# A linear-attention pass with weights loaded in place, statistics and residuals regrouped, and 1 + exp(-R) on ScalarE

## What is computed

```python
x = x + attn(layernorm(x))
# attn, with K, V, R = time_interp(x) @ W.T + b; 1024 channels
e  = exp(clip(-relu(decay) * t_rem + K, -20, 10));  eu = exp(clip(U + K, -20, 10))
A  = shift(cumsum(e * V)) + eu * V;  B = shift(cumsum(e)) + eu
out = (sigmoid(R) * A / B) @ Wo.T + bo
```

## Time and profile before

| | |
|---|---|
| median of 3 runs | 1482.85 us (1480.77 to 1484.4) |
| profiled execution | 1483.92 us, of which the span from first to last instruction is 1482.1 |
| TensorE matmuls busy | 1372.0 us (93%) |
| VectorE busy | 1198.0 us (81%) |
| ScalarE busy | 735.6 us (50%) |
| POOL busy | 624.6 us (42%) |
| mean granted clock of TensorE | 0.977 of full speed |

### The profile page before, as it was taken

One profiled execution on the slowest core, in us unless ns is written; L12 is line 12 of the kernel. 1 busy time (PEld: TensorE's weight loads), 2 busy tenths in 40 slices (PEclk: granted clock), 3 DMA queues, 4 the chain that ended last, 5 costly groups with the idle time before them and its releaser, 6 DMA issues. The chain is left out here.

```text
span 1482.1 us, 19289 instructions
## 1 busy us (share of the span) xinstructions
PE 1372.0 (93%) x6330; PEld 1115.8 (75%) x6330; DVE 1198.0 (81%) x1914; ACT 735.6 (50%) x1429; POOL 624.6 (42%) x520
## 2 busy tenths in 40 slices
PE   5678999999899998999999989999999889999998
PEld 4556788787787877878877678888888677777776
DVE  4678988998899988999899887777776687888874
ACT  4544555554555545555554434333335265555553
POOL 3433434343343333433434534444445444444452
PEclk9898999999999999999999999999999999999999
DMA  5112000100101001001031236444443312222212
GB/s 174 59 57 71 29 29 29 57 29 1 57 29 57 2 28 57 29 11 46 1 141 66 76 114 237 156 148 145 146 149 114 106 57 86 85 85 85 85 57 86
DMA packets 54549, 114.00 MB, mean 77 GB/s; under 512 B 2768, under 2 KB 7120, under 8 KB 52560
## 3 DMA queue, kind: packets, MB, share of 16 engines
q1 hardware_dynamic: 54480, 113.22, 21.7%
HBM read 88.05 MB, written 25.17 MB: 76 GB/s over the span
## 5 line engine op out<-in xcount | busy, mean ns | idle before, releaser
L779 POOL TENSOR_TENSOR a_ss<-a_ss,a_eu 128x512 f32<-128x512 f32 x64 | 82.5, 1290 | 369.1 <-DVE a_ss L590 369.1
L572 DVE SCALAR_TENSOR_TENSOR bank<-bank,k_or_row 128x510 f32<-128x510 f32 x192 | 132.4, 690 | 93.7 <-ACT k_or_row L458 93.7
L458 ACT ACTIVATE k_or_row<-bank 128x512 f32<-128x512 f32 x192 | 113.7, 592 | 47.3 <-PE bank L81 34.6
L784 POOL TENSOR_TENSOR a_sv<-a_sv,a_euv 128x512 f32<-128x512 f32 x64 | 82.4, 1288 | 111.8 <-DVE a_sv L604 111.8
L364 PE MATMUL bank<-a_wo_hi,a_y_hi 128*128 128x512 f32 x256 | 109.9, 429 | 18.3 <-DVE xres L651 18.3
L478 ACT ACTIVATE bank<-bank,a_nbr 128x510 f32<-128x510 f32 x64 | 42.3, 660 | 152.6 <-DVE bank L572 152.6
L364 PE MATMUL bank<-a_wo_lo,a_y_hi 128*128 128x512 f32 x256 | 105.3, 411 | 0.0
L364 PE MATMUL bank<-a_wo_hi,a_y_lo 128*128 128x512 f32 x256 | 105.3, 411 | 0.0
L488 ACT ACTIVATE bank<-a_ss 128x512 f32<-128x512 f32 x64 | 38.5, 602 | 101.0 <-DVE a_ss L615 101.0
L788 POOL TENSOR_TENSOR a_y_lo<-a_yy,a_y_hi 128x512 fp32r<-128x512 f32 x64 | 83.0, 1297 | 2.3 <-ACT a_y_hi L499 2.3
L1468 POOL TENSOR_TENSOR b_cx_lo<-b_cx,b_cx_hi 128x512 fp32r<-128x512 f32 x32 | 40.5, 1300 | 99.8 <-ACT b_cx_hi L1160 99.8
(11 more groups left out here) (241 smaller groups left out, 4729.3 us busy)
## 6 DMA issues: line engine op xcount, KB each, us to landing
xres<-in_x SPq DMA_DIRECT2D x8, 1024.0 KB, 5.2
x_after_attention<-xres SPq DMA_DIRECT2D x8, 1024.0 KB, 4.3
xin<-x_after_attention SPq DMA_DIRECT2D x8, 1024.0 KB, 5.6
b_ct<-in_ctx_t SPq DMA_DIRECT2D x8, 1024.0 KB, 4.8
b_cx<-in_ctx SPq DMA_DIRECT2D x8, 1024.0 KB, 7.7
xres<-x_after_attention SPq DMA_DIRECT2D x8, 1024.0 KB, 5.6
x_after_cross<-xres SPq DMA_DIRECT2D x8, 1024.0 KB, 4.4
xin<-x_after_cross SPq DMA_DIRECT2D x8, 1024.0 KB, 5.5
```

The lines of the kernel that those rows point to most:

```text
L458: sc.activation(u3[:, :, 1:], ps[m][:, :, :], ACT.Copy, scale=MIX[m]).then_inc(left[m], 1)
L572: ve.scalar_tensor_tensor(out=ps[m][:, :, 0:T - 1], in0=ps[m][:, :, 1:T], scalar=1.0 - MIX[m], in1=u3[:, :, 0:T - 1], op0=ALU.mult, op1=AL ...
L779: gp.tensor_tensor(ss3[:, :, 0:T], ss3[:, :, 0:T], eu[:, :, :], ALU.add).then_inc(b_done, 1)
L784: gp.tensor_tensor(sv3[:, :, 0:T], sv3[:, :, 0:T], euv[:, :, :], ALU.add).then_inc(a_done, 1)
```

## The change

- **Loads.** Each weight piece is loaded straight to the place where its rest part will stand (`w_raw` and `wo_raw` share the memory of the rest parts), so all 32 loads are issued without a wait. Four semaphores stand for chunks 0, 1, 2 to 3 and 4 to 7. The identity is now the first constant, the output bias moves behind the weights, then come the residual rows of tile 0, then the input of tile 1. Splits run two chunks ahead (`AHEAD`): chunk 1 before the loop, chunk c + 2 in chunk c, on ScalarE behind the eviction of R, on VectorE behind the denominator, on POOL (three of four) behind `y_rest`.
- **Statistics, residuals, normalisation.** All four statistics in chunk 0, the aggregate right behind `mix("k")` of chunk 1, all four residual rows at the end of chunk 1; `rstd_of` on POOL first in chunk 1; ScalarE normalises two rows in chunk 1 and two in chunk 2. TensorE waits for each residual row ahead of the matmuls that overwrite it.
- **1 + exp(-R)** becomes an Identity with bias 1.0 on ScalarE behind the two exps; the cap at 2^60 moves into the denominator. `weigh` is cut in two: eu V before `mix("r")`, e V after it.

```diff
@@ attention_pass, tiles and helpers
+        w_raw = {m: sh.slot(f"a_w{m}_raw", F32, 6 + 2 * j, 2) for j, m in enumerate(WM)}
+        wo_base = -(-nc.sbuf_base // 32) * 32
+        sb("wo", [P, 2, HC, C])
...
+        wo_raw = nc.alloc_sbuf_tensor_at("a_wo_raw", [P, HC, C], F32, offset=wo_base + HC * C * 4)
-        stage_in = [sem(f"stage_in{j}") for j in range(4)]
+        chunks_in = [sem(f"chunks_in{j}") for j in range(4)]
-        NCONST = 5
-        STAGED = 4 * HC
+        NCONST = 4
+        AHEAD = 2
+        def raw(n):
+            c, m = divmod(n, 4)
+            return (wo_raw if m == 3 else w_raw[WM[m]])[:, c, :]
+        def group(c):
+            return c if c < 2 else 2 if c < 4 else 3
+        def wait_piece(eng, n):
+            j = group(n // 4)
+            eng.wait_ge(chunks_in[j], 64 * (1, 1, 2, 4)[j])
@@ sync
-            for dst, src in ((col[:, :, :], cols), (trem_sb[:, :], trem), (mask_sb[:, :], scanmask),
-                             (id_sb[:, :], ident), (bo_sb[:, :], bo_b)):
+            for dst, src in ((id_sb[:, :], ident), (col[:, :, :], cols), (trem_sb[:, :], trem),
+                             (mask_sb[:, :], scanmask)):
                 sp.dma_start(dst, src).then_inc(consts_in, 16)
-            for n in range(STAGED):
-                if n >= 4:
-                    sp.wait_ge(wlo_done["kvro"[n % 4]], n // 4)
-                sp.dma_start(xres[:, n % 4, :], piece(n)[0]).then_inc(stage_in[n % 4], 16)
-                if n == 7:
-                    sp.wait_ge(turned, KC)
-                    sp.dma_start(xin[:, :, :], tile_of(x, 1)).then_inc(x_in, 16)
-            for m in "kvro":
-                sp.wait_ge(wlo_done[m], HC)
+            for n in range(4 * HC):
+                sp.dma_start(raw(n), piece(n)[0]).then_inc(chunks_in[group(n // 4)], 16)
+            sp.dma_start(bo_sb[:, :], bo_b).then_inc(res_in, 16)
             sp.dma_start(xres[:, :, :], tile_of(x, 0)).then_inc(res_in, 16)
+            sp.wait_ge(turned, KC)
+            sp.dma_start(xin[:, :, :], tile_of(x, 1)).then_inc(x_in, 16)
@@ tensor, output()
                 if c == 0:
-                    wait(pe, res_done, i * SUB)
...
                 for s in range(SUB):
+                    if c == 0 and not is_first(i):
+                        pe.wait_ge(res_done, i * SUB - SUB + s + 1)
@@ scalar
             def split_high(n):
-                act.wait_ge(stage_in[n % 4], 16 * (n // 4 + 1))
-                sc.activation(piece(n)[1], xres[:, n % 4, :], ACT.Copy).then_inc(whi_done, 1)
+                wait_piece(act, n)
+                sc.activation(piece(n)[1], raw(n), ACT.Copy).then_inc(whi_done, 1)
...
+                act.wait_ge(r_exp, 2 * g + 2)
+                sc.activation(ps["r"][:, :, :], ps["r"][:, :, :], ACT.Identity, bias=1.0).then_inc(t_done, 1)
...
             for k in range(KC):
                 xt_high(0, 0, k)
+            for n in range(4, 4 * AHEAD):
+                split_high(n)
...
-                    if is_first(i) and c < HC - 1:
-                        for m in range(4):
-                            split_high(4 * (c + 1) + m)
                     leave("k", g)
...
                     leave("r", g)
-                    if c == 2 and ahead:
-                        for s in range(SUB):
-                            normalise(i + 1, s)
+                    if is_first(i) and c < HC - AHEAD:
+                        for m in range(4):
+                            split_high(4 * (c + AHEAD) + m)
+                    if 1 <= c < 3 and ahead:
+                        normalise(i + 1, 2 * c - 2)
+                        normalise(i + 1, 2 * c - 1)
                     exp_r(g, c)
@@ vector
-            def one_plus(g):
-                dve.wait_ge(r_exp, 2 * g + 2)
-                ve.tensor_scalar(ps["r"][:, :, :], ps["r"][:, :, :], SIG_CAP, 1.0, ALU.min,
-                                 ALU.add).then_inc(t_done, 1)
...
-                ve.tensor_tensor(ss3[:, :, 0:T], ps["r"][:, :, :], ss3[:, :, 0:T], ALU.mult).then_inc(d_done, 1)
+                ve.scalar_tensor_tensor(out=ss3[:, :, 0:T], in0=ps["r"][:, :, :], scalar=SIG_CAP,
+                                        in1=ss3[:, :, 0:T], op0=ALU.min, op1=ALU.mult).then_inc(d_done, 1)
...
+            split_rest(0)
             for k in range(KC):
                 xt_rest(0, 0, k)
+            split_rest(4)
...
-                    split = is_first(i) and c < HC - 1
-                    if split:
-                        split_rest(4 * (c + 1))
+                    if c == 1 and ahead:
+                        dve.wait_ge(st_done, (i + 1) * SUB + SUB)
                     mix("k", g)
+                    if c == 1 and ahead:
+                        aggregate(i + 1)
...
-                    if c == 2 and not is_first(i):
-                        residual(i - 1, (2, 3))
-                    if split:
-                        split_rest(4 * (c + 1) + 3)
                     mix("v", g)
                     clip(g)
                     scan_e(g)
+                    weigh_own(g, c)
+                    mix("r", g)
                     weigh(g, c)
-                    mix("r", g)
                     scan_ev(g)
-                    one_plus(g)
                     if 3 <= c < 3 + KC and ahead:
                         xt_rest(i + 1, 1 - par, c - 3)
                     denominator(g)
-                    if c < 2 and ahead:
-                        statistics(i + 1, 2 * c)
-                        statistics(i + 1, 2 * c + 1)
-                    if c == 1:
-                        if ahead:
-                            dve.wait_ge(st_done, (i + 1) * SUB + SUB)
-                        if not is_first(i):
-                            residual(i - 1, (0, 1))
-                        if ahead:
-                            aggregate(i + 1)
+                    if is_first(i) and c < HC - AHEAD:
+                        split_rest(4 * (c + AHEAD))
+                    if c == 0 and ahead:
+                        for s in range(SUB):
+                            statistics(i + 1, s)
+                    if c == 1 and not is_first(i):
+                        residual(i - 1, range(SUB))
@@ gpsimd
             rstd_of(0)
-            for n in range(4):
-                split_rest(n)
-            pool.wait_ge(consts_in, 16 * NCONST)
+            for n in range(1, 4 * AHEAD):
+                if n % 4:
+                    split_rest(n)
...
-                    split = is_first(i) and c < HC - 1
-                    if split:
-                        split_rest(4 * (c + 1) + 1)
+                    if c == 1 and not is_last(i):
+                        rstd_of(i + 1)
                     below(g)
                     above(g)
                     if c > 0 or not is_first(i):
                         y_rest(g - 1, (c - 1) % HC)
-                    if split:
-                        split_rest(4 * (c + 1) + 2)
-                    if c == 1 and not is_last(i):
-                        rstd_of(i + 1)
+                    if is_first(i) and c < HC - AHEAD:
+                        for m in range(1, 4):
+                            split_rest(4 * (c + AHEAD) + m)
```

15 lines of the change are left out of this document (8 added, 7 removed).

## The result

The changed kernel takes 1417.31 us (median of 4 runs, 1415.12 to 1417.89) against 1481.81 for the kernel before (4 runs, 1477.63 to 1484.4): ratio 0.9565, 95% interval 0.9539 to 0.959. The profiled execution took 1417.16 us, its span is 1415.1; against the 1482.1 of before that is 67.0, and this is the number to account for.

A forecast was written before the change was run, and what follows sets the result against it. VectorE's loop was taken to bound attention's chunks, TensorE nearly as full, weights pacing tile 0. Savings of 22 (tiles 1 to 6), 22 (tile 0) and 2 (last tile), 46 off 1483.9, gave a median of 1437 us; range 1426 to 1462.

The forecast's parts named there:

- Two disturbances stay: ScalarE's 4.55 us of issue at the loop's back edge, twice.: Tiles 1 to 6: ScalarE's issue stall where the tile-pair loop goes round stays, charged 2 x 4.6 us.
- POOL's collisions in tile 0: Tile 0: POOL's three splits per chunk overlap VectorE's clips and split; 1.2 us charged for each of five chunks.
- x tile 1 lands at 40.: Tile 0: the second tile's input, queued behind all weights, arrives at 40 us at 333 GB/s; bounds 33 to 44.
- 91.3 per tile.: Tiles 1 to 6: VectorE's summed chunk times give 91.3 us per tile, about TensorE's 91.2 and 89.6.
- the collision in tile 1: Tile 1: one VectorE clip stretched to 1.52 us instead of 0.42 while POOL adds the bias; 1.1 charged.
- What attention saves they should pass on whole.: Passes after attention: same input and same waits, so no change of their own, 0 us.
- The last two: End of tile 0: the last two chunks take 10.6 to 11.0 us, in the sum ending the tile at 124.8.
- D: Rival, slower: denominator waits for 1 + exp, released T + 3.2 or later after mix("r") starts (T); T + 4 about 1490; chance 0.05.
- a new wait: Tile 0, chunk 0: VectorE, done at about 29, waits some 10 us for x tile 1 before its statistics.
- B: Rival: ordinary chunks get no shorter because ScalarE's Identity comes some 0.6 us late; 1460 us, chance 0.15.
- C: Rival: tile 0 gains half, as POOL's instructions hold VectorE's splits, clips and scans, about 12 us more; 1449, chance 0.14.
- E: Rival, no difference: tile 0's gain eaten by waiting for x tile 1, with ordinary chunks no shorter; 1483, chance 0.04.

The follow-up runs named there:

- e9: The kernel before with eight one-element copies added ahead of ScalarE's loop, the loop body unchanged; 1475.26 us.
- e10: The changed kernel with eight one-element copies added ahead of ScalarE's loop; 1419.02 us.
- part 1: 1 + exp on ScalarE, cap in the denominator, weigh cut in two; run alone on the kernel before: 1453.91 us, ratio 0.9819.
- e11: The changed kernel with x tile 1 loaded early, plus one of POOL's three splits per chunk in tile 0 moved between its two scan additions; 1410.83 us.
- Part 3: Weights loaded in place, splits two chunks ahead; run alone on the kernel before: 1453.45 us, ratio 0.9812.
- part 2: Statistics, aggregate, residuals, normalise and rstd regrouped, a wait per residual row; run alone on the kernel before: 1479.86 us, ratio 0.9991.

## Why the prediction was wrong, step by step

The sign, the mechanism of each part and every part's direction were right; the size was 20 us too small, and so the range missed. The terms that failed:

1. **"Two disturbances stay: ScalarE's 4.55 us of issue at the loop's back edge, twice."** This is the costliest step, 7.5 us: 9.2 were charged and 1.7 were found. It was a fetch of code, and the runs with instructions ahead of the loop show that eight more there remove it from the kernel before (e9) and bring half of it back in the changed one (e10). The row gave its length and not its cause; the prediction didn't read the queue of instruction packets, and kept the stall as if the change couldn't touch it. No case priced its going away; that alone would have moved the forecast to 1430.
2. **POOL's collisions in tile 0: 1.2 for each of five chunks, 6 in all.** Measured against chunks of 11.42 the middle four have 1.14 and three times 0.53, so 2.7. POOL's three splits reach the first clip only, and by about 0.5 to 1.1. Chunks 1 and 2 took 11.37 instead of 11.9 and 11.6, and with that this step makes some 4 us. The splits and normalises on ScalarE did delay the exp of chunk 1 by the 1.1 that was named: it comes 1.79 behind `mix("r")` instead of 0.72. First VectorE, then ScalarE:

```profile
45.48 0.69 DVE L591 SCALAR_TENSOR_TENSOR bank<-bank,k_or_row 128x510 f32<-128x510 f32 x1
...
48.73 0.69 DVE L632 SCALAR_TENSOR_TENSOR a_ss<-bank,a_ss 128x512 f32<-128x512 f32 x1 [0.66 <-ACT bank L498]
...
50.62 0.70 DVE L591 SCALAR_TENSOR_TENSOR bank<-bank,k_or_row 128x510 f32<-128x510 f32 x1 [0.56 <-ACT k_or_row L473]
```

```profile
47.27 0.64 ACT L493 ACTIVATE bank<-bank,a_nbr 128x510 f32<-128x510 f32 x1
```

The denominator waits 0.66 for it. But VectorE's own split then runs in what is the idle 1.19 of an ordinary chunk and leaves 0.56 of it, so the chunk pays for one of the two only. In chunk 2 the split takes 1.29 and fills that idle time whole, which costs nothing; the clip of 1.00, 0.58 too long, is paid.
3. **"x tile 1 lands at 40."** It landed at 36.5. The rate was the term: 333 GB/s came from 4 us of the kernel before, and while the queue is full here it moves 359 (the last number of the row):

```profile
2.00:36.00 34.00, 21.11 (x88) 17.41 (x88) 16.07 (x29) 17.71 (x34) 15.99 (x15) 1.00 1.02 359
```

12.3 MB at 359 take 34.2 us and not 36.9. The 2 for first issue was right (the first data move at 1.8), of the 1 for completion 0.4 was found. The landing was within its bounds (33 to 44) and gave 3.5 us: the second decay product came at 41.05 and not at 44.7.
4. **91.3 per tile.** It is 90.8: chunks with a turn take 11.42 and not 11.5, chunk 1 takes 11.71 and not 12.1, chunk 0 takes 12.18 and not 12.0. Over six tiles this is 3 us; the collision in tile 1 took back 0.9 (14.17 against 12.18, charged 1.1; it held two clips, at 1.30 and 1.52, and not one).
5. **"What attention saves they should pass on whole."** They added 3.6, within the range of this stretch over all kernels; whether part 1 has a share in it is open.

The sum: 7.5 + 7.7 (tile 0 ends at 122.8 and not 130.5) + 3.2 - 0.9 + 3.6 = 21.1, against 67.0 - 46 = 21.0. Two sums of the prediction are wrong in themselves. "The last two" chunks of tile 0 are one in its 124.8, which is right as a number. And D's time doesn't fit D's own threshold: if T + 3.2 eats the whole gain, T + 4 is 64 x 0.8 = 51 above 1483, some 1534 and not 1490.

What held: part 1 is hidden by ScalarE's idle time, with the slack that was named (product free at T + 2.2, predicted T + 2.3; the self-wait of the second scan takes the chain to 187.92 - 186.55 = 1.37, predicted 1.38). VectorE's loop is 10.60 without a turn. Odd and even tiles both take VectorE's time, 181.6 for a pair without the back edge; TensorE's own sum, 91.2 and 89.6, is 180.8, so it is only 0.8 below, and by these sums less work on VectorE would gain little more here. The residual wait of TensorE is gone, the clock is 1.00, and x tile 1 is a new wait. The chunks of 11.0 to 11.2 and 11.5 to 11.6 that the changed profile was to show are TensorE's, 10.97 to 11.18 and 11.42 to 11.64, and not VectorE's. The new wait was called 10 us and was 5.7, because VectorE got there at 30.7 and the data at 36.5. Behind chunk 1 of tile 0 the denominator has no wait.

The rivals. B (chunk no shorter) is out: 11.42 and 10.60. C (collisions take half of tile 0) is right in its mechanism for the clips and wrong in its price, since not even the 6 of the forecast were paid: the two scans average 1.23 over the whole pass in the changed kernel, since POOL's splits don't meet them there; e11 moves one into a scan, and it pays. D needed the product at T + 3.2; with the second Identity, which brings it 0.6 later to T + 2.8, the kernel is 28 us slower than without (some 3 of them the back edge) and still faster than before. E needed x tile 1 at 60.

One thing the prediction didn't say at all: the parts are unequal. Part 1 is worth 27 alone and 32 in place, and 8 to 9 of these are the back edge, most of which eight empty copies give the kernel before as well (2 x 3.3 in e9). Part 3 is worth 28 alone, part 2 nothing that can be told alone and 6.6 in place. Regrouping moves VectorE's work from one chunk to another and doesn't take any away; once part 1 had given VectorE slack ahead of TensorE, TensorE's wait for the residual rows was only 7.6 of the 18.3.

## What to carry to other kernels

An idle time that the profile puts down to "issue" at a loop's back edge isn't a constant of the kernel: any edit that adds or removes instructions ahead of the loop can remove it or bring it, so give it a case of its own, count the instruction packets of one pass beside it, and try a few empty instructions ahead of the loop. Here the line was drawn at three blocks of 128 instructions. Where one load ends a queue and one engine waits for it, move it ahead of what is needed later; here that was 6 us for three lines, and the version with it (1411.18) is faster than both kernels. Work moved to an idle engine is free only up to the slack of the one value it passes on: read that slack in one chunk, and double the work once to see it end.
